# A gated expert block whose first tiles come from a second sort: three stages instead of two, pads written on demand, a shorter choice

## The reference, cut to what matters

```python
x = _layernorm(x + _L0_attn_ref(x, Wq, Wk, Wv, Wo))              # attention, 4 sequences of 256
x = _layernorm(x + _L0_xattn_ref(x, token_ids, ctx, ctx, ctx))   # expert by token id: e = id // 3125
x = _layernorm(x + _L0_ffn_ref(x, Wr, br, Wg, Wu, Wd))           # top-1 of 4 experts by x @ Wr + br
# inside _L0_xattn_ref, for the expert e of the token's id:
y = (silu(h @ ctx[e].T) * (h @ ctx[e].T)) @ ctx[e]               # F = 256
# inside _L0_ffn_ref:
probs = softmax(x @ Wr + br); top_w, top_idx = top_k(probs, 1)
y = (silu(x @ Wg[e]) * (x @ Wu[e])) @ Wd[e]                      # F = 1024, e = top_idx
out = y * top_w
```

## Time and profile before

| | us |
|---|---|
| median of three runs | 195.73 |
| lowest and highest run | 194.76, 196.36 |
| the profiled execution | 194.84 |
| its span, first to last instruction | 192.5 |
| PE busy | 175.1 (91%) |
| DVE busy | 129.8 (67%) |
| ACT busy | 103.4 (54%) |
| POOL busy | 103.0 (53%) |

### The profile page before, as it was taken

The page is one execution under the profiler, slowest core; times in us unless marked ns, Lnnn a source line. Parts: engine busy times, 40 slices in busy tenths (PEclk is TensorE's granted clock), DMA queues, the critical chain, the costliest instruction groups (busy, mean ns, idle before and its releaser), DMA issues.

```text
span 192.5 us, 3892 instructions
## 1 busy us (share of the span) xinstructions
PE 175.1 (91%) x966; PEld 139.4 (72%) x966; DVE 129.8 (67%) x406; ACT 103.4 (54%) x274; POOL 103.0 (53%) x130
## 2 busy tenths in 40 slices
PE   1999999999999799989999999999999999999810
PEld 0877766367888546668888788888888888888610
DVE  3277878768687878536664454444799977888950
ACT  3138687535477654647664855534555423455530
POOL 7000267744917666528772368850688800376783
PEclk9999999999999999999999999999999999999975
DMA  5999999348997222247554005544050000011010
GB/s 163 354 334 418 376 364 346 102 140 232 353 371 295 93 87 64 74 116 215 171 167 163 0 1 177 171 156 158 0 167 0 0 0 3 0 54 60 22 63 24
DMA packets 15605, 29.14 MB, mean 151 GB/s; under 512 B 1758, under 2 KB 12000, under 8 KB 15458
## 3 DMA queue, kind: packets, MB, share of 16 engines
q1 hardware_dynamic: 13856, 25.68, 40.1%
q0 software_dynamic: 1440, 3.22, 4.7%
q10 hardware_dynamic: 290, 0.01, 0.1%
HBM read 20.41 MB, written 9.28 MB: 154 GB/s over the span
## 4 chain that ended last, share of the span: by engine, by line
PE 71%; POOL 11%; issue 7%; DVE 4%; DMA 3%; ACT 1%; POOLq 1%; DVEq 0%; ACTq 0%
PE bank L502 14%; PE bank L504 13%; PE bank L503 13%; POOL out_tokens L491 5%; PE bank L764 4%; PE bank L589 4%; PE bank L685 3%; PE bank L662 3%; POOL rstd L418 3%; PE bank L620 3%; PE bank L516 2%; PE bank L598 2%; PE bank L734 2%; PE bank L510 2%; DMA x_sorted<-buf,slot 1%
## 5 line engine op out<-in xcount | busy, mean ns | idle before, releaser
L414 POOL TENSOR_TENSOR w_lo<-stage,w_hi 128x512 fp32r<-128x512 f32 x40 | 51.3, 1303 | 34.7 <-ACT w_hi L841 29.9
L962 ACT ACTIVATE gate<-bank 128x256 f32<-128x256 f32 x44 | 16.9, 384 | 48.1 <-PE bank L504 48.0
L1264 DVE TENSOR_TENSOR hid<-bank,gate 128x256 f32<-128x256 f32 x44 | 18.7, 425 | 30.2 <-ACT gate L962 29.9
L502 PE MATMUL bank<-w_hi,xr 128*128 x88 | 35.9, 408 | 1.4 <-DVE xr L1217 1.2
L504 PE MATMUL bank<-w_hi,xr 128*128 x88 | 34.8, 395 | 0.0
L503 PE MATMUL bank<-w_lo,xr 128*128 x88 | 34.7, 395 | 0.0
L502 PE MATMUL bank<-w_hi,hT 128*128 x88 | 28.6, 324 | 0.7 <-DVE hT L1269 0.7
L418 POOL TENSOR_TENSOR rstd<-mv,mhalf 128x1 f32<-128x1 f32 x19 | 11.3, 597 | 31.2 <-DVE mv L1103 30.9
L841 ACT ACTIVATE w_hi<-stage 128x512 fp32r<-128x512 f32 x45 | 27.0, 630 | 0.3 <-PE bank L504 0.3
L504 PE MATMUL bank<-w_hi,hT 128*128 x88 | 24.9, 283 | 0.0
L503 PE MATMUL bank<-w_lo,hT 128*128 x88 | 24.8, 282 | 0.0
(11 more groups left out here) (188 smaller groups left out, 328.3 us busy)
## 6 DMA issues: line engine op xcount, KB each, us to landing
stage<-in_w_ffn SPq DMA_DIRECT2D x15, 768.0 KB
rows<-x_sorted SPq DMA_DIRECT2D x22, 132.0 KB, 2.2
x_sorted<-padrow SPq DMA_DIRECT2D x1, 2244.0 KB
x_sorted<-padrow SPq DMA_DIRECT2D x1, 2112.0 KB
buf<-in_x_tok SPq DMA_DIRECT2D x1, 1024.0 KB, 11.3
w_hi<-in_ctx SPq DMA_DIRECT2D x1, 1024.0 KB, 11.9
w_hi<-in_ctxT SPq DMA_DIRECT2D x1, 1024.0 KB
x_sorted<-padrow SPq DMA_DIRECT2D x1, 792.0 KB, 13.1
```

Source lines behind the costliest of these rows:

```text
L414: g.tensor_tensor(out=lo, in0=src, in1=hi.bitcast(F32), op=ALU.subtract).then_inc(split_lo, 1)
L502: mm(dst, xhi, whi, start=start, stop=False)
L962: a(gate[:, (T + j) % 2, :], fA[j % 2][:, 0:FQ], ACT.Silu).then_inc(silu_done, 1)
L1264: v.tensor_tensor(out=hid[:, (T + j) % 2, :], in0=fA[j % 2][:, FQ:2 * FQ], in1=gate[:, (T + j) % 2, :], op=ALU.mult).then_inc(h_done, 1)
```

## The change

- **Three stages.** Tiles 0-2 as before; tile 3 alone once nine tiles (`ROUTED = (7, 9, 11)`) have been ranked and scattered; tiles 4-10 with the rest. The tables of row numbers and of weight offsets are made apart: `row_tables` early, `offset_tables` later.
- **Pads on demand.** The two large DMAs go. One block of pads is written at the start; when all is ranked, DVE gives the end of each expert's rows (`pad_rows`), and SP writes one block of pads behind each, four DMAs whose place it reads into registers. Each expert's region is one block longer. Tile 3 doesn't wait for them, the later ones do.
- **Four-step choice.** The mask comes from a running maximum over the four logits and the token's mark (a large negative number for tokens, a large positive one for pads), compared with its end, and the difference of neighbours. The softmax's shifted logits are made later for all tiles at once (`shifted_logits`, in item 10). The norm's shift moves from ACT to DVE.
- **One-instruction roots.** POOL's addition of epsilon goes to DVE; POOL only makes the power.
- **New orders** on PE, DVE and ACT from tile 5 of stage 2 on to item 4 of the gated block.

The diff, cut to its core:

```diff
+ROUTED = (7, 9, 11)
+MIDDLE = EARLY + 1
@@ SP
-            pads2 = scr2.rearrange("(p r) c -> p r c", p=P)
-            HALF2 = BLOCKS2 // 2
-            sp.dma_start(pads2[:, 0:HALF2, :], padrow[:].unsqueeze(1).broadcast_to([P, HALF2, ROW])).then_inc(d_init2, 16)
+            sp.dma_start(scr2[(BLOCKS2 - 1) * P:BLOCKS2 * P, :], padrow[:]).then_inc(d_pads, 16)
...
             for t in range(EARLY):
                 routed_row(t, r[t])
+            sp.wait_ge(d_pads, 16)
+            sp.wait_ge(pad_table, 1)
+            r = [sp.value_load(pad_from[0:1, e:e + 1], ...) for e in range(E)]
+            for e in range(E):
+                sp.dma_start(scr2[bass.ds(r[e], P), :], padrow[:]).then_inc(d_pads, 16)
             sp.wait_ge(row_table, 2)
-            r = {t: first_row(t) for t in range(EARLY, EARLY + 2)}
-            sp.wait_ge(d_scat2[1], 16 * (T - ROUTED))
-            for t in range(EARLY, T):
+            r = first_row(EARLY)
+            sp.wait_ge(d_scat2[1], 16 * (ROUTED[1] - ROUTED[0]))
+            routed_row(EARLY, r)
+            sp.wait_ge(row_table, 3)
+            r = {t: first_row(t) for t in range(MIDDLE, MIDDLE + 2)}
+            sp.wait_ge(d_pads, 16 * (1 + E))
+            sp.wait_ge(d_scat2[2], 16 * (ROUTED[2] - ROUTED[1]))
+            for t in range(MIDDLE, T):
@@ POOL
-            validity()
+            move_tokens()
             root2(0)
+            scatter2(0)
             root2(1)
-            pool.wait_ge(d_init2, 32)
-            for t in range(0, 3):
-                scatter2(t)
+            scatter2(1)
+            scatter2(2)
             root2(2)
@@ PE, stage 2 and ahead of stage 3
-                if i == 7:
-                    rank(0)
-                if i == 9:
-                    rank(1)
+                if i == 10:
+                    rank(2)
                 if 2 <= i:
                     down(i - 2)
-                if i == 10:
-                    rank(2)
-            idle_products(12)
+                if i == 6:
+                    rank(0)
+                if i == 8:
+                    rank(1)
+            idle_products(13)
             rank(3)
-            idle_products(6)
+            idle_products(5)
@@ PE, stage 3
             ftx(0)
             rank(4)
+            ftx(1)
+            idle_products(3)
+            fup(0)
+            ftx(2)
+            fup(1)
+            fth(0)
+            fup(2)
+            fth(1)
+            fdown(0)
+
+            ftx(3)
+            fth(2)
+            fdown(1)
+            pe.wait_ge(tables, 3)
+            fup(3)
+
+            ftx(4)
+            fdown(2)
+            fth(3)
+            ftx(5)
+            pe.wait_ge(tables, 4)
+            fup(4)
@@ ACT
-            SHIFT_AT = {6: 0, 9: 1, 10: 2}
-            NORMS_AT = {7: (0, 1), 8: (2,), 9: (3, 4), 10: (5, 6)}
+            NORMS_AT = {6: (0, 1), 7: (2,), 8: (3,), 9: (4, 5), 10: (6,)}
@@ DVE, choose(n)
-                step(v.tensor_tensor(out=logit, in0=lm, in1=rstd2, op=ALU.mult))
-                step(v.tensor_tensor(out=logit, in0=logit, in1=br_all, op=ALU.add))
-                step(v.tensor_reduce(out=lmax, in_=logit, op=ALU.max))
-                step(v.tensor_tensor(out=lm, in0=logit, in1=lmax, op=ALU.subtract))
-                step(v.scalar_tensor_tensor(out=lw, in0=lm, scalar=0.0, in1=prio2, op0=ALU.is_ge, op1=ALU.mult))
-                step(v.tensor_reduce(out=lwmax, in_=lw, op=ALU.max))
-                v.tensor_tensor(out=m2, in0=lw, in1=lwmax, op=ALU.is_equal).then_inc(mask_ready, 1)
+                v.scalar_tensor_tensor(out=nmr2, in0=mean, scalar=-1.0, in1=rstd2, op0=ALU.mult, op1=ALU.mult).then_inc(nmr2_ready, 1)
+                for t in range(a, b):
+                    v.scalar_tensor_tensor(out=choice[t], in0=logits[t], scalar=rstd2[t], in1=br_all, op0=ALU.mult, op1=ALU.add).then_inc(logit_ready, 1)
+                dve.wait_ge(logit_ready, b)
+                step(v.tensor_tensor_scan(out=run, data0=cap, data1=choice, initial=LOW, op0=ALU.min, op1=ALU.max))
+                step(v.tensor_tensor(out=at_max, in0=run, in1=run's last, op=ALU.is_equal))
+                v.tensor_tensor(out=m2, in0=at_max[1:], in1=at_max[:-1], op=ALU.subtract).then_inc(mask_ready, 1)
@@ DVE, order from tile 10 of stage 2 to item 0
+            place(2)
+            hidden(10)
+            residual_moments(7)
             early_tables()
-            residual(9)
-            residual(10)
+            residual(8)
+            evicted_moments(9)
+            evicted_moments(10)
             choose(3)
+            offset_tables(0, EARLY)
             place(3)
+            middle_whole()
             choose(4)
+            middle_flags()
             fxlo(0)
+            pad_rows()
+            middle_table()
             place(4)
             fxlo(1)
-            late_tables()
+            middle_chosen()
+            late_flags()
+            fhidden(0)
+            late_table()
```

363 lines of the change are left out of this document (202 added, 161 removed).

## The result

The changed kernel took 200.44 us, median of four runs (200.28 to 200.52), beside 195.69 us (194.76 to 196.36) for the kernel before: ratio 1.0237, 95% interval 1.0207 to 1.0267. The forecast was 195.9 us with a range from 193.2 to 197.7, so it was wrong. Two more measurements of the same changed kernel, on other occasions, gave 197.40 us (ratio 1.0127, 1.0085 to 1.0169) and 198.05 us (1.0149, 1.0112 to 1.0186); the first of these lies inside the range, the second outside. Both facts need a cause: that it is slower by more than 1% by all three medians, and that on the first occasion it was slower by another 1%. Medians here are over all runs of a kernel, ratios and intervals only over those within 1.5% of its fastest.

A forecast was written before the change was run, and what follows sets the result against it. It took PE to bound the gated block, leaving 2.4 us of stalls between the second stage's last tiles and item 5 to win. 194.84 - 0.55 + 0.75 - 0.4 + 1.3 = 195.9 us, range 193.2 to 197.7.

The forecast's parts named there:

- Two more steps in the gates: Gates in the gated block: the added steps lie in DVE's pauses of 1.2 us an item, so cost nothing.
- Pads: SP's queue ahead of tile 3's row: loads and writes take 4.4 us, row issued at 78.6, nothing lost below.
- third: the offset tables: DVE behind item 2's gate: both tables take 1.1 us before tile 3's low part; item 3 at 83.3 against 83.54.
- The choice and the third group: Second stage: choices 0.35 us shorter, the 1.07 us mask wait goes, first rows 1.7 us earlier, which reaches nothing.
- Late next, first: Last tile's second product waits for tile 8's sum behind the early tables; item 0 still starts 0.55 us earlier.
- Second: the late table: DVE ahead of tile 2's low part: 1.2 us of late row table puts item 2 at 78.55 against 78.33.
- Fourth: two splits: ACT: tile 4's high part waits behind item 3's two weight splits; item 5 starts 1.1 us later, at 88.95.
- the clock below 1.00: Sign that the forecast is wrong: a granted clock below 1.00 between 68 and 90 us, with the longer waits.
- tile 3's row after 82 us: Sign that the forecast is wrong: tile 3's row landing after 82 us, where 80.8 was forecast.
- the 2.3 us around the span: Whole execution: the forecast counted from the earlier profiled execution, 194.84 us for a span of 192.5.
- Rival B: SP's queue: pads end after 80.3, each us goes straight into item 3; over 1% slower, 197.5 us; chance 0.18 with other late rows.

The follow-up runs named there:

- b1: The kernel before, with its single token conversion in the gates replaced by the changed kernel's two token steps: 195.93 us, ratio 1.0052.
- the repeat: The changed kernel measured again without edits on a second occasion: 197.40 us, ratio 1.0127 to the kernel before; its profiled run took 197.49 us.
- e16: e15 with tile 8's sum also put ahead of the early tables on DVE: 195.28 us, ratio 1.0016 to the kernel before.
- e10: Changed kernel with offset tables moved, token steps one item later, and tile 4's high part ahead of item 3's two splits on ACT: 195.89 us, ratio 1.0042.
- e19: e16 with the pads again ahead of tile 3's row in SP's queue: 195.27 us, ratio 1.0023 to the kernel before.
- e21: e20 with six idle products added on PE ahead of tile 3's turn: 195.81 us, ratio 1.0022 to the kernel before.
- e18: e17 with nine idle products added on PE ahead of tile 3's turn: 198.65 us, ratio 1.019 to the kernel before.
- e17: Changed kernel with two more register loads on SP behind the pads' four: 199.12 us, ratio 1.0203 to the kernel before.
- e20: e19 with item 4's first products ahead of item 3's transposes on PE: 194.70 us, ratio 0.9995 to the kernel before.
- e1: Changed kernel with the two old large pad blocks put back in place of the small pad loads and writes: 199.91 us, ratio 1.027.
- e8: Changed kernel with both the old large pads put back and the two offset tables moved: 199.20 us, ratio 1.021.
- e4: Changed kernel with the two token steps of the gates called one item later on DVE: 196.61 us, ratio 1.013.
- e15: e10 with the pads behind tile 3's row on SP and the late table behind tile 2's low part: 196.26 us, ratio 1.0063.

## Why the prediction was wrong, point by point

**Two more steps in the gates "lie in DVE's pauses": this step failed.** It priced them at nothing and they cost 1.0 us, because they wait for low parts on POOL. The trace of before held the warning. The single conversion there took 0.66 us for 11 numbers, and ended (110.44) with POOL's first low part of 1.27 us (110.40):

```profile
109.13 2.54 POOL L414 TENSOR_TENSOR w_lo<-stage,w_hi 128x512 fp32r<-128x512 f32 x2 [6.90 <-ACT w_hi L841]
109.78 0.66 DVE L1289 CAST outidx<-rows 128x11 int32<-128x11 f32 x1
```

b1 shows the cost in full.

**"Pads" and "third: the offset tables": mis-sized.** Loads and writes were put at 4.4 us, and tile 3's issue at 5.0 us behind the pads' start; in the repeat it is 6.0 (74.21 to 80.19), in the first profile 6.9. The first step of the first offset table was put at 0.2 us and took 1.15, again a wait for POOL, here in the repeat:

```profile
81.52 1.26 POOL L434 TENSOR_TENSOR w_lo<-stage,w_hi 128x512 fp32r<-128x512 f32 x1 [1.28 <-ACT w_hi L866]
81.69 1.15 DVE L1228 TENSOR_TENSOR arena<-arena,off_step 128x32 f32<-128x32 f32 x1
```

The two are late together: the row lands at 82.35 and the tables end at 83.78, so in the repeat item 3 waits 0.53 us for DVE after 1.19 for the row. Instead of 0.46 us gained between items 2 and 3, 0.44 was lost; 0.9 in all. On the first occasion the chain of waits went through SP's loads, in the repeat through DVE's table. Shares by line of the chain from 74 to 92 us, first profile, then repeat:

```profile
by line: issue 16.4%; SPq L360 11.9%; DMA rows<-x_sorted 11.9%; PE bank L516 9.8%; SPq L362 8.4%; PE bank L518 8.2%; PE bank L517 7.9%; ACT w_hi L866 6.3%; DVE xr L1284 4.8%; SPq L348 3.6%; PE bank L748 2.4%; ACT xr L970 1.6%; DVE nth L1039
```
```profile
by line: PE bank L516 18.4%; PE bank L518 13.8%; PE bank L517 13.5%; DVE arena L1228 9.9%; DVE xr L1284 6.7%; ACT w_hi L866 6.3%; issue 6.2%; DVE hid L1336 4.7%; ACT gate L975 4.5%; PE bank L524 3.6%; DVE off L1242 3.2%; DVE arena L1348 1.8
```

**The choice and the third group: right.** The mask wait of 1.07 us ahead of the third group's ranking is gone, and the last choice took 1.09 us from its shift to its mask (73.41 to 74.50) where 1.05 was forecast. It reached nothing, as said.

**"Late next, first": right place, wrong size.** A wait ahead of the last tile's second product was forecast at 0.9 us and is 0.82. But item 0 was to gain 0.55 and lost 0.12 by distance. e16 puts what this order holds back at 1.1 us. **"Second: the late table"** cost 0.2 us and not 0.75; its sum with the first, 0.2 forecast against 0.33, is nearly right by luck.

**"Fourth: two splits": right size, wrong cause.** Forecast 1.36 us between items 3 and 5, measured 1.31. But e10 moved the splits and gave back 0.24 there. The order of the work, with item 3's transposes ahead of item 4's products and ACT and DVE to match, holds 0.34: from e19 to e21 items 3 to 5 went from 5.18 to 4.84. The rest of the gap to 4.29 was not found.

**The clock was named only as a sign that the forecast is wrong, and had no price.** Two of these signs came on the first occasion: the clock below 1.00, and tile 3's row after 82 us (84.4). By distances the repeat lies 2.0 us beyond the forecast: 1.0 from the tokens, 0.9 from tile 3, 0.1 from the others together. In time it lies only 1.6 beyond (197.49 against 195.9), because the forecast took over the 2.3 us around the span and they became 2.0; that gain was luck. The first result (200.4) lies another 2.9 beyond, from the lower clock behind tile 3 (1.15), the later row (0.55) and the start (1.15), which differs from run to run. Rival B had the right mechanism at 0.18. Its price, "each us goes straight into item 3", was wrong both ways: in e18 a row issued 0.9 us later moved item 3 by 0.45, since the tables were late beside it, and in e17, with the same row, the clock cost 1.27 more.

## What to carry to other kernels

A small operation that takes three times its like in the trace of before is waiting for something; ask what runs beside it before putting more operations in that place. When a chain is shortened, list what is issued on every queue between the old and the new place: here four register loads and four writes stood in the sync engine's queue, and a table on DVE was just as late beside them, so undoing the pads alone gained nothing and both together a microsecond. Compare profiles by distances between fixed points, not by absolute times, and measure a kernel on more than one occasion before giving a difference of 1% a cause.

## What the runs showed of the hardware

- The granted clock fell to 0.50 (1.2 GHz) behind stands of PE of 1.53, 1.58, 1.71, 1.85, 2.03 and 2.07 us (e20, b1, e1, e8, e17, first profile) and not behind 1.19, 1.25, 1.29, 1.44 and 1.45 (the repeats, e4, e15, e16), the start of the program left out. In the gated block the low clock cost 1.0 to 1.35 us each time, by the distance from item 3 to item 4. Idle products in the place of the stand kept it at 1.00 (e18, e21). By their times it did not fall in every run of e17 and e20, but only one run of each was profiled.
- DVE steps with two inputs in SBUF, and conversions of numbers in SBUF, waited for the end of a running GpSimd operation (0.66, 0.67, 0.92, 1.15 and 1.21 us in place of 0.2). A reduction and a reciprocal beside it took their usual 0.19 and 0.23 us, and so did steps of which one input is a bank of PSUM (0.41 to 0.42 us).
- Four register loads on the sync engine took 2.45 to 2.65 us in ten profiles and 3.66 in one, with the same instructions around them. Two more loads made it 3.7 (e17, e18).
- The second stage began up to 1.9 us apart from run to run. Between the first profile and the repeat (1.15 us) the difference lies in when PE's matmuls at the start go from 0.43 us apart to half of that: from 8 to 10 us it did 6 and 16. The granted clock reads 1.00 for those two microseconds in both, so the granted clock as recorded does not explain it.
